# A hybrid block on one core: SiLU products one loop unit later, the first transposes inside the output projection, a third gate tile between products of the scan's preparation

## The reference, cut to what matters

```
x = x + rwkv(layernorm(x))      # linear attention with a recurrence over tokens
x = x + ffn(layernorm(x))       # "F1": silu(x Wg) * (x Wu), times Wd; inner width 1376
x = x + mamba(layernorm(x))     # "M": projection to 1024 + 1024 (x part and gate), causal convolution
                                #   over 4 tokens, silu -> u; u Wx -> dt (128), B (16), C (16);
                                #   delta = softplus(dt Wdt + b)
                                #   h = h * exp(delta * A) + delta * u * B   (1024 channels x 16 states)
                                #   y = sum over states of h * C, plus u * D
                                #   out = (y * silu(gate)) Wo
x = x + ffn(layernorm(x))       # "F2": the same weights as F1
```

## Time and profile before

| | |
|---|---|
| median of 3 runs | 3488.43 us (3487.74 to 3488.74) |
| the profiled execution | 3486.4 us, its span 3484.6 us |
| TensorE matmuls busy | 3204.3 us, 92% |
| VectorE busy | 3133.7 us, 90% |
| ScalarE busy | 2609.9 us, 75% |
| GpSimd busy | 2485.7 us, 71% |
| chain that ended last | GpSimd 48%, issue 21%, VectorE 16%, TensorE 7% |
| VectorE's products of the FFN (line 1372) idle ahead for ScalarE | 130.0 us in 76 waits, over all steps and the tail |
| mean granted TensorE clock | 0.965 of 2.4 GHz |

### The profile page before, as it was taken

How to read it: one execution, slowest core, us unless ns; L and a number is a source line. 1 busy time by engine, 2 the same in 40 slices (tenths; PEclk the granted TensorE clock), 3 DMA queues, 4 the chain that set the end, 5 groups by cost and what they waited for, 6 DMA issues and landing times.

```text
span 3484.6 us, 46858 instructions
## 1 busy us (share of the span) xinstructions
PE 3204.3 (92%) x12704; PEld 2325.5 (67%) x12704; DVE 3133.7 (90%) x5676; ACT 2609.9 (75%) x5276; POOL 2485.7 (71%) x1964
## 2 busy tenths in 40 slices
PE   6898989899999999999999999999999999976738
PEld 5666766676777767676767676767677777754525
DVE  7998984699999999999999999999999999999990
ACT  6777773687888887878887887878787878776740
POOL 1444444396969696969696969697979697968680
PEclk9999999999999999999999999999999999988869
DMA  3222223111111111111121112121211120111110
GB/s 115 67 85 83 72 67 116 58 37 38 43 38 43 41 40 41 41 40 46 37 47 34 47 34 52 28 55 26 57 25 55 25 55 25 55 26 36 28 34 6
DMA packets 119381, 165.39 MB, mean 47 GB/s; under 512 B 8544, under 2 KB 84192, under 8 KB 118624
## 3 DMA queue, kind: packets, MB, share of 16 engines
q1 hardware_dynamic: 119136, 162.63, 16.8%
HBM read 128.39 MB, written 25.69 MB: 44 GB/s over the span
## 4 chain that ended last, share of the span: by engine, by line
POOL 48%; issue 21%; DVE 16%; PE 7%; ACT 4%; DMA 3%; DVEq 1%; POOLq 0%; SPq 0%; ACTq 0%
POOL dBu L938 26%; POOL yacc L951 17%; DVE D L1454 5%; DVE U L1403 4%; PE W L1195 3%; DMA BC<-bc_scratch 2%; DVE prod L1475 1%; PE W L1229 1%; POOL NV L314 1%; DVE D L1478 1%; POOL EO L302 1%; DMA bc_scratch<-bcS 1%; POOL MX L287 1%; DVE qX L668 1%; POOL MX L285 1%
## 5 line engine op out<-in xcount | busy, mean ns | idle before, releaser
L938 POOL TENSOR_TENSOR dBu<-U,BC 128x512 f32<-128x512 f32 x1024 | 1308.6, 1291 | 334.0 <-DMA BC<-bc_scratch 330.4
L1454 DVE TENSOR_TENSOR_SCAN D<-D,hc,dBu 128x256 f32<-128x256 f32 x2048 | 1446.5, 750 | 19.5 <-ACT D L1110 19.4
L1195 PE MATMUL W<-nT,wffn 128*128 128x256 f32 x5632 | 1229.4, 381 | 6.9 <-ACT nT L979 6.9
L1195 PEld LDWEIGHTS W<-nT,wffn 128*128 128x128 f32 x5632 | 1061.6, 189 | 181.1 <-issue 13.4
L1110 ACT ACTIVATE D<-delta,A 128x256 f32<-128x256 f32 x2048 | 891.5, 468 | 350.8 <-DVE yacc L1488 329.7
L951 POOL TENSOR_TENSOR yacc<-yacc,prod 128x512 f32<-128x512 f32 x752 | 957.5, 1273 | 165.7 <-DVE prod L1475 161.2
L1229 PE MATMUL W<-wffn,hT 128*128 128x512 f32 (+1 forms) x1408 | 617.5, 594 | 8.3 <-DVE hT L1372 8.3
L1475 DVE TENSOR_TENSOR prod<-D,BC 128x512 f32<-128x512 f32 x752 | 513.8, 683 | 0.1
L1229 PEld LDWEIGHTS W<-wffn,hT 128*128 128x128 f32 (+1 forms) x1408 | 262.8, 190 | 327.1 <-issue 307.8
L1195 PE MATMUL W<-nT,win 128*128 128x256 f32 x2048 | 452.4, 382 | 30.2 <-ACT xext L1027 22.9
L1195 PEld LDWEIGHTS W<-nT,win 128*128 128x128 f32 x2048 | 391.9, 192 | 92.1 <-ACT xext L1027 23.7
(11 more groups left out here) (133 smaller groups left out, 2981.1 us busy)
## 6 DMA issues: line engine op xcount, KB each, us to landing
BC<-bc_scratch SPq DMA_DIRECT2D x256, 256.0 KB, 4.7
XM<-x_scratch SPq DMA_DIRECT2D x29, 512.0 KB, 6.1
X<-x_scratch SPq DMA_DIRECT2D x17, 512.0 KB, 3.6
ix<-idx SPq DMA_DIRECT2D x33, 255.0 KB, 2.9
X<-x SPq DMA_DIRECT2D x16, 512.0 KB, 3.4
XR<-x SPq DMA_DIRECT2D x16, 512.0 KB, 3.4
x_scratch<-XR SPq DMA_DIRECT2D x16, 512.0 KB, 3.6
out<-X SPq DMA_DIRECT2D x16, 512.0 KB, 2.7
```

The costliest lines, as they stand in the source:

```text
L938: nc.gpsimd.tensor_tensor(dBu[e % 4][:], U[:, 2 * j:2 * j + 2, :], BC[slot][:, 0:1, :].to_broadcast([P, 2, CH]), ALU.mult).then_inc(s_dBu, 1)
L1195: last = T_.matmul(dst, lhsT, rhs, start=(n == 0), stop=(n == len(terms) - 1))
L1454: V.tensor_tensor_scan(D[:, m, :], D[:, m, :], dBu[e % 4][:, m % 2, :], hc[:, n, m:m + 1], ALU.mult, ALU.add).then_inc(s_scan, 1)
```

## The change

Three edits: `MULT` goes from -1 to 0, so that each `gated` product of an FFN stands one unit later in VectorE's loop. TensorE issues gate tile 6 ahead of the wait for the fourth pair of U, and only tile 7 behind the products with Wdt. In the steps that have both F1 and a projection, the wait for `m_sg` and the eight transposes of F1 stand in the middle of the projection of token half 1 (after 4 of its 8 tiles) and no longer ahead of it. In the other steps their order is as it was.

```diff
-MULT = -1
+MULT = 0
-EARLY_GATES = 2
+EARLY_GATES, MIDDLE_GATES = 2, 1
@@ project
-                def project(i, t, side):
+                def project(i, t, side, halfway=None):
 ...
                     for k in range(ME):
+                        if halfway and k == ME // 2:
+                            halfway()
                         last = T_.matmul(o[:, t, :], sgm[i % 2][:, k, t * P:(t + 1) * P], wo[:, k, :], start=(k == 0), stop=(k == ME - 1))
@@ step of TensorE
                     for q in range(ME // 2):
+                        if q == ME // 2 - 1:
+                            gate(1, 4 + EARLY_GATES, 4 + EARLY_GATES + MIDDLE_GATES)
                         pe.wait_ge(m_u, 4 * i + q + 1)
 ...
-                    gate(1, 4 + EARLY_GATES, 8)
+                    gate(1, 4 + EARLY_GATES + MIDDLE_GATES, 8)
                     pe.wait_ge(m_sg, 2 * i + 1)
                     if back:
                         project(i - 1, 0, b)
                     mamba = norm_no("M", i + 1) if more else None
                     F, L = ffn_no(*late(i)), norm_no(*late(i))
-                    pe.wait_ge(m_sg, 2 * i + 2)
+
+                    def first_turn():
+                        pe.wait_ge(m_sg, 2 * i + 2)
+                        turn(norm_no(*early(i)) if f1 else L, side_early(i))
+
+                    if f1 and back:
+                        project(i - 1, 1, b, first_turn)
+                    else:
+                        if back:
+                            project(i - 1, 1, b)
+                        first_turn()
                     if f1:
                         E_, L_ = ffn_no(*early(i)), norm_no(*early(i))
-                        turn(L_, side_early(i))
-                        if back:
-                            project(i - 1, 1, b)
                         ffn(E_, L_, side_early(i), (m_res, i), L)
                         ffn(F, L, side_late(i, f1), (f_res, E_ + 1), mamba)
                     else:
-                        project(i - 1, 1, b)
-                        turn(L, side_late(i, f1))
                         ffn(F, L, side_late(i, f1), (m_res, i), mamba)
```

## The result

The changed kernel takes 3520.96 us (median of 4 runs, 3518.62 to 3524.47) against 3488.09 us of the kernel before in the same job: ratio 1.0097, 95% interval 1.0084 to 1.0110. It is 33 us slower; the forecast was 3505 us, and the time lies 1 us above the range of 3484 to 3520.

What follows compares the result with a forecast made beforehand. TensorE and VectorE, both nearly full, bound the kernel in turn, with TensorE pacing the step. Periods 11.3, clock loss 1.7, step 0 1.7 and later fourth pair there 1.7 were summed to 16.4 us: 3505 us, range 3484 to 3520.

Steps and rivals of the forecast that it cites:

- ahead of the transposes: TensorE's wait for the second gate SiLU before F1's transposes: 0.35 us left of 2.09.
- for the copy: TensorE's wait before F1 for ScalarE's copy of the transposed rows: 0.8 us.
- ahead of F1's down products: TensorE's wait for VectorE's product of group 4 in F1: 2.65 us instead of 0.58.
- ahead of F2's: TensorE's wait before the down products of F2: 1.1 us where it waited 0.
- the residuals: VectorE's waits for TensorE at its FFN residuals: about 1.5 us in F1, about 0.9 us in F2.
- TensorE comes from behind to the fourth pair: At the fourth pair of U, TensorE arrives late without idle time, so the gate tile delays it by 1.74 us.
- The loop from one fourth pair to the next: One step's chain alternating between TensorE and VectorE: 172.8 us against 171.93, +0.9 us a period.
- I take one such loss in the 13: Clock drop behind the pause before F1's down products, in one of 13 periods: +1.7 us, bounds 0 and 22.
- much slower: Rival: the 2.65 us pause drops the clock in nearly every step, or ScalarE takes over removed waits: 3525 us, chance 0.13.
- Step 0: Entry into step 0: the tile costs its whole 1.7 us, fourth pair at 826.8 instead of 825.08.
- Steps 14 and 15: The last steps, with slack on TensorE: taken as 0 us, bounds -1 and +1.
- the gate tile alone: Third gate tile ahead of the fourth pair of U, without the other edits: costs 0.2 to 1.05 us a period.

Runs made afterwards that it cites:

- e5: Changed kernel plus ten short filler matmuls, results thrown away, in the pause ahead of the down products of F1 alone, steps 1 to 13: 3507.10 us.
- e2: Changed kernel without the third gate tile, which goes back behind the Wdt products: 3498.06 us.
- e8: Kernel before with the third gate tile ahead of the fourth pair of U alone: 3516.05 us.
- e7: Kernel before with the transposes of F1 moved within the projection alone: 3463.31 us.
- e10: Kernel before with the earlier down products and the transposes within the projection, `MULT = -1`, no third gate tile: 3462.51 us.
- e9: Kernel before with the earlier down products, the transposes within the projection and `MULT = 0`, no third gate tile: 3435.30 us.
- e3: Changed kernel without the later products (`MULT = -1`), keeping the transposes within the projection and the third gate tile: 3477.19 us.
- e4: Changed kernel with token half 0's down products started after SiLU 4, only tiles 8 and 9 waiting for group 4's product: 3446.48 us.
- e11: Kernel before with the earlier down products alone: 3484.70 us.
- e6: Kernel before with the products one unit later (`MULT = 0`) alone: 3518.97 us.

## Why the prediction missed

**What held.** The mechanism, and nearly every wait of it. Waits ahead of the transposes 0.36 us (predicted 0.35), for the copy 0.66 (0.8), ahead of F1's down products 2.6, in one period 3.0 (2.65), ahead of F2's 1.30 (1.1), the residuals in periods without a loss 1.5 (1.5) and 1.8 (0.9), no wait for the fourth pair, no wait of VectorE for a SiLU in these periods. The loop from one fourth pair to the next was worked out as 172.8 us, and 172.9 were measured once the clock was kept out of it (e5). It isn't a sum of errors that cancel: from F1's down products to F2's the TensorE rows of the changed kernel have 1827.78 - 1768.47 = 59.3 us, where the prediction has 20.07 + 39.0 + 0.06 = 59.1, and from there to the fourth pair 1876.91 - 1827.78 = 49.1, where it has 46.43 + 0.87 + 1.74 = 49.0. That TensorE comes from behind to the fourth pair, so that the tile delays it: 1.3 us a clean period (e5 against e2), where the sum has the whole 1.74.

**What failed.** One term: "I take one such loss in the 13 (+1.7; bounds 0 and 22)". There were 9, worth 14.4 us by e5 against the profile of the changed kernel; with them the sum of 16.4 us would have been 29, against 33 measured. The rival "much slower" had this mechanism and the time 3525 us, with a chance of 0.13 for it and another cause together; that chance was too small. The two rows on which the choice rested, 2.93 us with a loss and 2.61 without, were single cases, and they were read as an edge in the length of the pause. The same trace speaks against an edge: of the two pauses of 3.00 us in stage one the first was followed by matmuls at a granted clock of 1.00, the second at 0.81.

```profile
207.76 7.13 PE L466 MATMUL trP<-wo,yT 128*128 128x512 f32 x16 [3.00 <-POOL yT L293]
...
474.90 8.83 PE L466 MATMUL trP<-wo,yT 128*128 128x512 f32 x16 [3.00 <-POOL yT L293]
```

And stage two had its losses in 5 of 13 steps at a pause of 2.09 us. A pause of 2.6 us in each of 13 steps should have been given more than one. Which of the 13 get a loss, at pauses of the same length, no run here explains.

**Smaller.** Step 0 cost 2.8 instead of 1.7 us, and the first stage of the profiled execution was some 3 us later without any change in its code; the runs' medians have 33 us where the spans have 35. Steps 14 and 15 came to 0.6 us where 0 was taken. And the prediction priced the gate tile alone at 0.2 to 1.05 us a period; alone it costs 2.05 (e8, 173.98 against 171.93), with a pause of 3.79 us ahead of the transposes and a clock loss in all 13 periods instead of 5.

**Where the gain went.** The transposes alone win 22 us (e7). The later products give that back and more: 3463 becomes 3498 (e7 to e2), 34 us when each is taken against its own kernel before, since the down products wait for the product of group 4. With that wait moved behind eight of its tiles the same edit wins 27 us (e10 to e9). So the edit's sign hangs on an order on another engine. The tile costs 31 us alone (e8), 21 on top of the two (e2 to the changed kernel), 14 on top of the transposes (e7 to e3) and 10 on top of both and the earlier down products (e9 to e4): it never paid.

## What to carry to other kernels

Where two engines are both nearly full, a period is a chain that goes back and forth between them; write it down from one fixed point to the same point a step later, and a moved instruction is worth what it does to that chain and not what its own wait was. Before delaying a product, look at what its reader really needs of it: here a wait for a whole group stood ahead of eight tiles that didn't need it. And count a pause on TensorE twice, once as idle time and once for the clock behind it, in each step in which it comes: in the 13 periods of these kernels the clock fell at some of the pauses of 1.9 us and more and at none of 1.8 us or less.

## What the runs showed of the hardware

TensorE's clock at pauses that return in every step, by what was measured: at 3.79 us and the eight transposes behind it, losses in 13 of 13 periods (e8); at 2.06 to 2.09 us and the transposes, 5 of 13 (before and e11) and 9 of 13 (e6); at 2.6 us without transposes 9 of 12, and none behind the one of 2.97 (changed); at 2.4 us 7 of 13 (e2); at 1.9 us 1 of 11, and none behind one of 2.0 and one of 2.3 (e3); at 1.7 to 1.8 us none of 13 (e7). A loss costs 1.4 to 1.7 us (e8 has no period without one to compare with). The length of a pause doesn't decide alone: in the changed kernel the one of 2.97 us had no loss behind it and the next, 2.61 us, had. Ten instructions with results that nobody reads, put into the pause, prevented the losses in all 13 periods (e5) and paid 14 us in the profiled execution, 11 in the medians, for no useful work; removing the pause paid 72 (e4).
